# Fewer, smaller first loads for an attention stage, and an attention mask written to PSUM as four 64x64 tiles

## The reference, cut to what matters

```python
# layer 0, attention: 16 heads of 8, relative positions clipped at 128
scores = jnp.einsum('bhqd,bhkd->bhqk', q, k)
scores = scores + jnp.einsum('bhqd,qkd->bhqk', q, rel_pos)
attn = jax.nn.softmax(scores / np.sqrt(8), axis=-1)
...
# layer 1, gate block: DEPTH = 6, 16 heads of 64, windows of 32 queries that see 64 keys
mask = (it < jb) | (it > jb + w) | (jb == -1)
sim = jnp.einsum('bhwie,bhwje->bhwij', bq, bk2) * QK_SCALE
sim = jnp.where(mask, -jnp.finfo(sim.dtype).max, sim)
attn = jax.nn.softmax(sim, -1)
```

## Time and profile before

| what | value |
|---|---|
| median of 3 runs | 4047.76 us (4047.39 to 4051.94) |
| profiled execution, its time | 4043.93 us |
| its span, first to last instruction | 4041.2 us |
| mean granted TensorE clock | 0.870 of full speed |
| TensorE busy over the span | 80% |
| first attention, first maximum to the last score tiles | from 123 us to 809 us |
| transformer, first to last mask matmul | 2007.6 us to 3982.8 us |

### The profile page before, as it was taken

How to read it: one execution, slowest core, us unless ns; L and a number is a source line. 1 busy time by engine, 2 the same in 40 slices (tenths; PEclk the granted TensorE clock), 3 DMA queues, 4 the chain that set the end, 5 groups by cost and what they waited for, 6 DMA issues and landing times. The chain is left out here.

```text
span 4041.2 us, 71890 instructions
## 1 busy us (share of the span) xinstructions
PE 3229.5 (80%) x23909; PEld 1685.1 (42%) x23909; DVE 2296.0 (57%) x3463; ACT 2100.1 (52%) x3805; POOL 1069.5 (26%) x967
## 2 busy tenths in 40 slices
PE   2578788724960499997399999999999999999997
PEld 1213223111330133332166556556556655655654
DVE  6677677755232477776655545555554554555553
ACT  1355555511210166665166666666666666666664
POOL 0000000001420211111255435434444533543541
PEclk6576666756985599999699999999999999999998
DMA  5222212222428111111311111111111111111111
GB/s 187 68 48 52 63 36 52 48 57 51 107 53 44 24 24 24 28 27 42 100 42 49 32 45 50 31 47 39 46 43 38 49 32 45 53 32 44 39 39 38
DMA packets 192098, 198.89 MB, mean 49 GB/s; under 512 B 114369, under 2 KB 121145, under 8 KB 186970
## 3 DMA queue, kind: packets, MB, share of 16 engines
q1 hardware_dynamic: 154396, 192.23, 18.7%
q10 hardware_dynamic: 37344, 1.97, 1.0%
HBM read 98.98 MB, written 28.81 MB: 32 GB/s over the span
## 5 line engine op out<-in xcount | busy, mean ns | idle before, releaser
L2376 POOL TENSOR_TENSOR tr_t<-tr_t 128x512 f32<-128x512 f32 x384 | 489.0, 1273 | 707.3 <-DVE tr_t L2220 707.3
L2383 POOL TENSOR_TENSOR tr_nq<-tr_t,tr_rn 128x512 f32<-128x512 f32 x384 | 392.6, 1044 | 401.7 <-ACT tr_rn L2116 401.7
L1595 DVE TENSOR_REDUCE attn_mp<-attn_ps 128x1 f32<-128x512 f32 (+3 forms) x660 | 395.5, 657 | 161.8 <-PE attn_ps L1446 86.5
L2081 ACT ACTIVATE tr_pr<-tr_ps 128x768 f32<-128x768 f32 x264 | 213.9, 810 | 385.0 <-PE tr_ps L1903 383.9
L2219 DVE TENSOR_TENSOR tr_t<-tr_ps,tr_tab 128x512 f32<-128x512 f32 x384 | 263.6, 686 | 243.2 <-ACT tr_sq L2090 243.2
L678 DVE TENSOR_REDUCE attn_mcol<-attn_ps 128x1 f32<-128x1024 f32 x274 | 333.2, 1222 | 116.3 <-PE attn_ps L526 115.4
L1918 PE MATMUL tr_ps<-tr_w,tr_xs 128*128 128x512 f32 x768 | 371.2, 605 | 29.1 <-DVE tr_xs L2247 24.7
L2229 DVE TENSOR_TENSOR tr_o<-tr_ps,tr_rd 128x384 f32<-128x384 f32 (+1 forms) x264 | 144.1, 546 | 438.9 <-ACT tr_rd L2106 438.0
L1557 ACT ACTIVATE attn_pr<-attn_ps 128x768 f32<-128x768 f32 (+2 forms) x352 | 300.9, 870 | 166.8 <-PE attn_ps L1479 163.8
L663 ACT ACTIVATE attn_pr<-attn_ps 128x512 f32<-128x512 f32 x512 | 279.6, 597 | 206.9 <-DVE attn_ps L692 200.1
L1903 PE MATMUL tr_ps<-tr_qT,tr_kT 64*128 64x96 f32 (+1 forms) x4224 | 300.8, 282 | 0.0
(11 more groups left out here) (259 smaller groups left out, 5185.1 us busy)
## 6 DMA issues: line engine op xcount, KB each, us to landing
tr_v<-tr_va SPq DMA_DIRECT2D x144, 192.0 KB, 2.5
attn_ka<-scratch_kp SPq DMA_DIRECT2D x72, 288.0 KB, 6.1
tr_v<-tr_va SPq DMA_DIRECT2D x144, 128.0 KB, 2.5
moe_cb<-scratch_combineT SPq DMA_DIRECT2D x32, 512.0 KB
tr_w<-in_w_half SPq DMA_DIRECT2D x12, 1024.0 KB
tr_v<-tr_va SPq DMA_DIRECT2D x48, 256.0 KB, 2.4
scratch_kp<-proj_parts SPq DMA_DIRECT2D x36, 256.0 KB
attn_qg<-scratch_qp SPq DMA_DIRECT2D x10, 784.0 KB
```

The lines of the kernel that those rows point to most:

```text
L1595: dve.tensor_reduce(dst, src, AX.X, ALU.max).then_inc(maxed, 1)
L2376: pool.tensor_tensor(t12[:, slot, i, 0, :], t12[:, slot, i, 0, :], t12[:, slot, i, 1, :], ALU.add).then_inc(summed, 1)
L2383: pool.tensor_tensor(nq[:, slot, i, :].rearrange("p (h e) -> p h e", e=DH), t12[:, slot, i, 0, :].rearrange("p (h e) -> p h e", e=DH), rn[ ...
```

## The change

It has two parts.

In the first attention, bound and maximum share contraction row 48: `max_tile` reads the bound there, and `load_rows` later overwrites it with the negated maximum of the same head. `NK` becomes 49. `ka` is loaded with 49 rows, the last of which is ones for all three variants of k (the projection stores two more rows of ones), and the constants `fixed` and `fixed_rows` go. `relp` is stored in the form in which `relpack` wants it, so that two loads replace twelve. The first group's q is loaded as four pairs of heads instead of all eight at once, after the keys of head 0, and TensorE waits for a pair's q before its first tile; for `relpack` and the rest it waits after tile 17. In the transformer, the mask is written by four matmuls of 64x64 tiles instead of two of 128x128: `band` gets a second copy with the halves of its rows exchanged, and a semaphore increment that nobody waits for takes the step's waits.

```diff
@@ stage_project0, sync @@
-            sp.dma_start(d["kp"][0, 0:B * H0, KROWS, :], ones[0:B * H0, :]).then_inc(stored, 16)
-            n += 1
+            for v in range(3):
+                sp.dma_start(d["kp"][v, 0:B * H0, KROWS, :], ones[0:B * H0, :]).then_inc(stored, 16)
+                n += 1
...
-            sp.dma_start(d["relp"].rearrange("v e c -> e v c"), relparts[:]).then_inc(stored, 16)
+            for blk in range(NPACK):
+                sp.dma_start(d["relp"][blk * HD:(blk + 1) * HD, :], relparts[:, KPART[blk], :]).then_inc(stored, 16)
+                n += 1
@@ first attention @@
-MAXROW = KROWS + 1
-NK = KROWS + 2
+NK = KROWS + 1
...
                     for r in first_row:
-                        sp.dma_start(ka[r:r + KROWS, slot, e, :, :],
-                                     d["kp"][:, 2 * n + e, 0:KROWS, :].rearrange("v r s -> r v s")
+                        sp.dma_start(ka[r:r + NK, slot, e, :, :],
+                                     d["kp"][:, 2 * n + e, :, :].rearrange("v r s -> r v s")
                                      ).then_inc(ka_loaded[slot], 16)
...
-                        sp.dma_start(qg[r + MAXROW:r + MAXROW + 1, buf, 2 * p + e, :].rearrange("o (u i) -> o u i", i=P),
+                        sp.dma_start(qg[r + KROWS:r + KROWS + 1, buf, 2 * p + e, :].rearrange("o (u i) -> o u i", i=P),
                                      mrow[e * ST:(e + 1) * ST, p % 2, :]).then_inc(rows_loaded[p % 2], 16)
...
-            load_q(0, 0)
             load_km(0, 0)
-            load_km(1, 1)
+            for h in range(0, GH, 2):
+                for r in first_row:
+                    sp.dma_start(qg[r:r + NK, 0, h:h + 2, :], d["qp"][h:h + 2, :, :].rearrange("h r s -> r h s")
+                                 ).then_inc(q_first[h // 2], 16)
+                if h == 0:
+                    load_km(1, 1)
             for r in first_row:
-                for blk in range(NPACK):
-                    sp.dma_start(relpack[r + blk * HD:r + (blk + 1) * HD, :], d["relp"][KPART[blk]]
-                                 ).then_inc(consts, 16)
-                for slot in range(2):
-                    sp.dma_start(km[r + MAXROW:r + MAXROW + 1, slot, :], d["fixed"][0:1, 0:S]).then_inc(consts, 16)
-                    for e in range(2):
-                        sp.dma_start(ka[r + KROWS:r + KROWS + 2, slot, e, :, :],
-                                     d["fixed"].rearrange("o (v s) -> o v s", s=S)).then_inc(consts, 16)
-                sp.dma_start(qg[r + MAXROW:r + MAXROW + 1, :, :, :].rearrange("o a h s -> o (a h s)"),
-                             d["fixed_rows"]).then_inc(consts, 16)
+                sp.dma_start(relpack[r:r + KROWS, :], d["relp"]).then_inc(consts, 16)
             load_ka(0, 0)
             load_ka(1, 1)
             next_km(0, 2)
...
-            pe.wait_ge(consts, 16 * NCONST)
-            pe.wait_ge(q_loaded[0], 32)
             for m in range(LEAD):
+                if m % (2 * ST) == 0:
+                    pe.wait_ge(q_first[m // (2 * ST)], 32)
                 max_tile(0, 0, m)
+            pe.wait_ge(consts, 16 * 2)
+            for x in range(GH // 2):
+                pe.wait_ge(q_first[x], 32)
@@ stage_transformer @@
-        band32 = st.sb("band32", [P, 2, NPAIR * QT])
-        band = st.sb("band", [P, 2, NPAIR * QT], BF16)
+        band32 = st.sb("band32", [P, 2, 2, NPAIR * QT])
+        band = st.sb("band", [P, 2, 2, NPAIR * QT], BF16)
...
-            sp.dma_start(band32[:], d["band"]).then_inc(loaded_const, 16)
+            sp.dma_start(band32[:, 0, :, :], d["band"]).then_inc(loaded_const, 16)
+            for half in range(2):
+                sp.dma_start(band32[half * DH:(half + 1) * DH, 1, :, :], d["band"][(1 - half) * DH:(2 - half) * DH]
+                             ).then_inc(loaded_const, 16)
...
                 pe.wait_ge(qk_ready, 2 * (NTT * n + tile) + 2)
+                pe.sem_inc(scores_begun, 1)
                 for e in range(2):
-                    pe.matmul(ps[:, SC0 + e, 0:NPAIR * QT], identb[:], band[:, 1 if s == 0 else 0, :], start=True,
-                              stop=True)
+                    for half in range(2):
+                        row, out = half * DH, (half ^ e) * DH
+                        pe.matmul(ps[out:out + DH, SC0 + e, 0:NPAIR * QT], identb[row:row + DH, row:row + DH],
+                                  band[row:row + DH, e, 1 if s == 0 else 0, :], start=True, stop=True,
+                                  tile_position=(row, out), skip_group_check=True)
...
-            dve.wait_ge(loaded_const, 64)
+            dve.wait_ge(loaded_const, 96)
             link(dve.tensor_copy(band[:], band32[:]))
```

More of the change, by code:

```diff
@@ L210, in _ @@
             sp.wait_ge(rel_split, 1)
-            sp.dma_start(d["relp"].rearrange("v e c -> e v c"), relparts[:]).then_inc(stored, 16)
+            for blk in range(NPACK):
+                sp.dma_start(d["relp"][blk * HD:(blk + 1) * HD, :], relparts[:, KPART[blk], :]).then_inc(stored, 16)
+                n += 1
             sp.dma_start(d["x_stash"][1], qT[:]).then_inc(stored, 16)
-            n += 2
+            n += 1
             for v in range(4):
@@ L375, in stage_attention0 @@
         q_loaded = [st.sem("q_loaded0"), st.sem("q_loaded1")]
+        q_first = [st.sem(f"q_first{x}") for x in range(GH // 2)]
         km_loaded = [st.sem("km_loaded0"), st.sem("km_loaded1")]
@@ L389, in stage_attention0 @@
         rel_rows = [slice(r, r + KROWS) for r in first_row]
-        NCONST = 2 * (NPACK + 2 * 3 + 1)
         @block.sync
@@ L482, in _ @@
                 sp.wait_ge(km_loaded[slot], 32 * (GH // 2 * NG + 2))
-                sp.wait_ge(q_loaded[slot], 32 * (NG // 2 + 1 - slot))
+                sp.wait_ge(q_loaded[slot], 32 * (NG // 2))
         @block.gpsimd
@@ L523, in max_tile @@
                 if m == TILES:
-                    pe.wait_ge(q_loaded[1 - s], 32 * ((g - s) // 2 + 1 + s))
+                    pe.wait_ge(q_loaded[1 - s], 32 * ((g - s) // 2 + 1))
                 for c in range(2):
@@ L1801, in stage_transformer @@
         summed, nq_ready, turned, qk_ready = S_("summed"), S_("nq_ready"), S_("turned"), S_("qk_ready")
-        scores_done, exp_done = S_("scores_done"), S_("exp_done")
+        scores_done, exp_done, scores_begun = S_("scores_done"), S_("exp_done"), S_("scores_begun")
         v_done, v_copied = S_("v_done"), S_("v_copied")
@@ L2580, in host_arrays @@
     a["ident"] = np.eye(P, dtype=np.float32)
-    fixed = np.zeros((2, 3 * S), mybir.dt.np(BF16))
-    fixed[1] = 1
-    a["fixed"] = fixed
-    a["fixed_rows"] = np.zeros((1, 2 * GH * S), mybir.dt.np(BF16))
     a["headsel"] = np.repeat(np.eye(H0, dtype=np.float32), HD, axis=0)
@@ L2599 @@
     "kp": ([3, B * H0 + 4, KROWS + 1, S], BF16),
-    "relp": ([3, HD, CH], BF16),
+    "relp": ([KROWS, CH], BF16),
     "x_stash": ([2, P, T], F32),
```

## The result

The kernel after takes 4033.03 us (median of five runs, 4029.00 to 4039.16) against 4047.76 before (five runs, 4044.12 to 4051.94). The ratio is 0.9964 with a 95% interval of 0.9949 to 0.9979; the forecast was 4027, in a range of 3984 to 4070. Timed again later beside the kernel before, the same kernel gave 0.9956 (0.9941 to 0.9972). The gain of 15 to 18 us is short of the 21 forecast. One execution among all those timed for this document, of the kernel with the new mask alone, took 5467.8 us at a mean granted clock of 0.57 and stands outside every ratio.

What follows compares the result with a forecast made beforehand. TensorE's own time was taken to bound the transformer, and a chain from the first window the first attention. -13 + 2 - 10 = -21 on a 4041.2 us span gave 4020, an execution of 4023, median 4027; range 3984 to 4070.

Steps and rivals of the forecast that it cites:

- Start of the attention, -13: First attention: first window at 129.3 us instead of 142.47, held by head 2's keys; -13 us, bounds -20 and -8.
- head 2's keys are in time: Rival at the first attention's start: keys land near 121, first window at 122, -20 us, total 4020; chance 0.12.
- a shift of that window shifts all behind it: First attention: from its first window the stage waits for no load, so the whole -13 us reaches the end.
- The second keys: nothing: Rest of the first attention: 49-row loads of the second keys cost nothing, with 18 us of cover.
- 1.7 for the narrow loads: First attention's start: at 48-row speed the second keys' 2.41 MB would pass 1.7 us sooner than with 49 rows.
- Stores and constants: nothing: Extra stores of ones and relp: their 2 to 3 us on SP are hidden by its wait, costing nothing.
- Start of the transformer, +2.2: Transformer's start: larger load and cast of `band` delay TensorE's first matmul by 2.2 us, bounds +1.2 and +3.6.
- +1.2: Transformer's start: the cast of `band`, 1.23 us before, doubles and adds 1.2 us.
- +1.0: Transformer's start: the `band` load brings 384 KB more and takes 1.0 us longer.
- The mask, -10: Transformer, 264 steps: four tiles at once take 0.29 us against 0.326; -10 us, bounds -20 and +4.
- The case of two or three rounds: Rival in the transformer's mask: tiles take turns; two rounds total 4069, chance 0.17; three rounds 4112, chance 0.07.
- The case that only contraction rows count as a shape: Rival between mask and scores: no change of shape there, -0.16 us a step, -42 us, total 3985; chance 0.08.

Runs made afterwards that it cites:

- e3: Kernel after with head 2's keys issued ahead of the eight loads of the second keys: 4036.68 us, ratio 0.9967 to the kernel before.
- e4: Kernel after with the mask on 64 contraction rows and 128 columns, two rounds of two matmuls: 4020.81 us, ratio 0.9927 to the kernel before.
- e1: Kernel before with only the new first attention, the mask unchanged: 4042.64 us, ratio 0.9975 to the kernel before.
- e5: Kernel after with head 2's keys issued earlier and the mask in two rounds of 64 rows by 128 columns: 4012.39 us, ratio 0.9902 to the kernel before.
- e9: Kernel after with each load of the second keys cut in two, 48 rows and 1 row: one run, 4041.22 us.
- e10: Kernel before, unaltered, profiled again: single execution, 4057.25 us.
- e11: Kernel before, unaltered, profiled once more for the spread: single execution, 4050.75 us.
- e8: Kernel after with the two 128x128 mask matmuls of before but the added increment kept: first to last mask 1973.8 us, no total time given.
- e2: Kernel before with only the new mask, the first attention unchanged: 4043.8 us, ratio 0.9985 to the kernel before.
- e6: Kernel after, unaltered, timed again for a second profile: 4038.04 us, ratio 0.9956 to the kernel before.
- e12: Kernel before with only the new mask, profiled once more: single execution, 4033.34 us.

## Why the prediction was right, and where it was off

**Start of the attention, -13: right in its place, about half of it in the time.** First maximum 103.76 (forecast 103, with 1.3 us for the report of the last bytes there and 1.0 for head 2's keys; no row shows either), tile 16 at 127.29 released by a DMA of keys (128.5), first window 128.10 (129.3), DMA share 0.46 to 0.49. The alternative that head 2's keys are in time is refuted by the trace of after, and e3 makes it come true. The step that failed is the last sentence on what bounds the kernel: "a shift of that window shifts all behind it". It holds for the waits; the length of the stage also moved with its clock, which the sentence leaves out. Taking the transformer's part out of each timed ratio shows how much reached the end. That part is -10 + 2 for the tiles and -30 + 2 for the masks of e4. Over a kernel of 4050 us, e1 leaves -10 for the start, after -7 and -10, and e4 -2, where the first window moved by 14 to 15; e3 leaves -5 and e5 -12 where it moved by 20. Each is uncertain by some 5 us, and they are not independent (e1, e3 and e4 are compared with the same runs of before), but together they are about half of the shift. That is most of the miss of 6 us in the median. That the other half went to a lower clock fits the profiles; it is not shown, and the cause of a lower clock stays open.

**The second keys: nothing, right,** with 3 us instead of 1.7 for the narrow loads at the start (e9), where they delay head 2's keys. **Stores and constants: nothing,** no wait on them shows.

**Start of the transformer, +2.2: right in sum, wrong in its parts.** From the issue of the load before the band's (`tr_cols_all`, at 1975.57 before and 1975.00 after) to TensorE's first matmul it takes 14.2 us before and 16.45 after, +2.3; it is 14.2 in all four profiles with one copy of `band` (before, e1, e10, e11) and 15.5 to 17.1, 16.2 in the mean, in the ten with two. But the cast of twice the columns took 0.96 us where the old one took 1.23, and not +1.2; the three loads in place of one made it start 2.5 later, and not 1.0. The prediction took the old cast for one that waits for its load alone. In its four profiles the small cast took 1.23, 1.52, 1.62 and 1.68 us, started while GpSimd was still clearing `tr_o`, and ended 0.41 us after GpSimd each time, so by these four profiles its end was set by GpSimd, and not by its start or its columns. The large one started 0.7 to 2.3 us after GpSimd was done and took 0.96 (0.95 in e4 and e5). That a wrong +1.2 and a wrong +1.0 add up to the right +2.2 is luck.

**The mask, -10: right.** First to last mask matmul is 1975.2, 1978.9, 1973.8, 1977.6 and 1973.3 us with 128x128 masks (before, e1, e8, e10, e11), and 1967.9, 1967.2, 1963.7, 1965.0, 1964.4 and 1963.5 with the four tiles (after, e2, e6, e3, e9, e12): 1975.8 against 1965.3 in the mean. The 0.09 of idle, the 0.163 of columns and the start of the scores at 0.29 are as forecast; the increment is free (e8). The case of two or three rounds is refuted twice, by the four starts within about 0.01 us and by the doubled tiles, which add 0.16 and not 0.3. The Trainium skill (TensorEngine Tiling (Array Packing), Gotcha 1: PSUM Pressure) says that different row tiles cannot access one PSUM bank simultaneously; here each of the two banks is written by two row tiles at once, on different partitions, and they take no turns. The measurement decides. The case that only contraction rows count as a shape is refuted too, by e4: with the scores' own shape the idle time ahead of them goes, though the change from bfloat16 to float32 is still there, and with 64x64 tiles it stays.

## What to carry to other kernels

Count a change of tile shape on TensorE as a cost: ahead of the first matmul of the new shape stood 0.09 us here, and its first weight load was partly uncovered, so matmuls put next to each other in one shape can win more than matmuls split to run side by side (-30 us for two rounds in the scores' shape, -10 for one round in a shape of its own). A small load that the next work waits for is issued ahead of the large ones on its queue. And a time won ahead of a stage in which the clock is throttled is not yet won at the end: read the granted clock of that stage in several profiles before a forecast is worked out from one. Before a VectorE instruction's length goes into a sum, look whether GpSimd is at work beside it: the cast here was set by that and not by its columns.

## What the runs showed of the hardware

- The granted clock of one stage differed between executions of the same program: 0.67, 0.64 and 0.65 in the first attention of before (666.3, 679.4 and 674.9 us), 0.64 and 0.61 of after (679.8 and 691.2).
- Four 64x64 tiles on the four quarters of the array, two banks each written from both row halves, take the time of one: 0.16 us for 384 bfloat16 columns.
- Eight loads of 288 or 294 KB kept the DMA engines busy 1.08 (before) and 0.91 (e9) of the time with 48 partitions and 0.46 with 49 (after), and the rate moved far less: 181 and 186 GB/s against 175.
- A cast by VectorE of 128x768 elements that started during a GpSimd memset took 1.23 to 1.68 us and ended 0.41 us after the memset in four of four profiles; one of 128x1536 with GpSimd idle took 0.95 or 0.96 in ten.
